# Row moments of a second normalisation, taken by ScalarE and GpSimd instead of VectorE, inside a top-k attention kernel

## What is computed

```python
x = x + attention(layernorm(x))      # 16 heads of 64, relative positions, top 32 scores of each row kept
x = x + ffn(layernorm(x))            # base product + low-rank experts gated by a softmax

def _layernorm(x, axis=-1, eps=1e-05):
    m = jnp.mean(x, axis=axis, keepdims=True)
    v = jnp.var(x, axis=axis, keepdims=True)
    return (x - m) / jnp.sqrt(v + eps)

# in attention, for each head:
top_vals = jax.lax.top_k(scores, TOPK)[0]          # TOPK = 32
threshold = top_vals[..., -1:]
scores = jnp.where(scores < threshold, -jnp.inf, scores)
attn = jax.nn.softmax(scores, axis=-1)             # then three powers of attn times v, weighted by alphas
```

## Time and profile before

| | us |
|---|---|
| median of 3 runs | 708.71 |
| lowest, highest | 706.1, 710.16 |
| the profiled execution, its own time | 707.67 |
| its span, first to last instruction | 705.7 |

### The profile page before, as it was taken

How to read it: one execution, slowest core, us unless ns; L and a number is a source line. 1 busy time by engine, 2 the same in 40 slices (tenths; PEclk the granted TensorE clock), 3 DMA queues, 4 the chain that set the end, 5 groups by cost and what they waited for, 6 DMA issues and landing times.

```text
span 705.7 us, 20962 instructions
## 1 busy us (share of the span) xinstructions
PE 655.9 (93%) x5780; PEld 510.2 (72%) x5780; DVE 676.5 (96%) x2813; ACT 619.9 (88%) x1774; POOL 552.6 (78%) x985
## 2 busy tenths in 40 slices
PE   4378999999999999999999999999999999999796
PEld 3256777777777777877777777777777777777664
DVE  6899999999999999999999999999999999999963
ACT  3678999989999899999999999998999999998753
POOL 1588898888878888888887888788887888888740
PEclk9779999999999999999999999999999999999999
DMA  6644444544554545454544544454545444545212
GB/s 202 189 117 145 143 142 147 149 123 144 165 156 140 149 135 154 135 154 137 152 137 139 151 144 146 132 157 134 155 126 163 135 139 145 151 136 154 69 47 59
DMA packets 148338, 98.72 MB, mean 140 GB/s; under 512 B 10624, under 2 KB 147968, under 8 KB 148096
## 3 DMA queue, kind: packets, MB, share of 16 engines
q1 hardware_dynamic: 147920, 97.32, 47.0%
q10 hardware_dynamic: 304, 0.08, 0.1%
HBM read 45.59 MB, written 51.77 MB: 138 GB/s over the span
## 4 chain that ended last, share of the span: by engine, by line
DVE 79%; issue 9%; PE 7%; POOL 2%; ACT 2%; DMA 1%; ACTq 0%; DVEq 0%; POOLq 0%; SPq 0%
DVE top L749 41%; DVE work L755 36%; PE ps_p L974 2%; DVE rinv L736 1%; POOL s_sb L331 1%; PE ps_y L994 1%; ACT a_sb L491 1%; DMA x_sb<-in_x 0%; DMA band_scratch<-band 0%; DVE stats L771 0%; PE ps_d L951 0%; PE ps_qk L896 0%; PE ps_p L920 0%; PE ps_d L942 0%; DMA skew<-band_scratch 0%
## 5 line engine op out<-in xcount | busy, mean ns | idle before, releaser
L749 DVE MAX8 top<-work 128x8 f32<-128x256 f32 x768 | 286.8, 418 | 0.0
L755 DVE MATCH_REPLACE8 work<-top,work 128x256 f32<-128x256 f32 x512 | 207.3, 416 | 0.0
L331 POOL TENSOR_TENSOR s_sb<-s_sb,pen 128x512 f32<-128x512 f32 x127 | 162.0, 1276 | 38.6 <-ACT pen L481 35.5
L336 POOL TENSOR_SCALAR a_sb<-a_sb,rinv 128x256 f32<-128x256 f32 x254 | 118.7, 478 | 53.0 <-DVE rinv L736 52.7
L491 ACT ACTIVATE a_sb<-s_sb,nmax 128x256 f32<-128x256 f32 x256 | 128.2, 502 | 27.9 <-POOL s_sb L331 19.2
L481 ACT ACTIVATE pen<-s_sb,limit 128x256 f32<-128x256 f32 x254 | 116.3, 511 | 19.7 <-POOL limit L318 19.6
L306 POOL TENSOR_TENSOR s_sb<-s_sb,skew 128x384 f32<-128x384 f32 x128 | 128.4, 1003 | 2.5 <-DMA skew<-band_scratch 2.5
L974 PE MATMUL ps_p<-aT,rows 128*64 128x256 f32 x1024 | 125.3, 386 | 0.4 <-ACT rows L555 0.2
L755 DVE MATCH_REPLACE8 work<-top,s_sb 128x256 f32<-128x256 f32 x256 | 103.6, 415 | 0.0
L749 DVE MAX8 top<-s_sb 128x8 f32<-128x256 f32 x256 | 95.1, 416 | 3.9 <-POOL s_sb L306 3.9
L882 PE MATMUL ps_a<-ident,a_sb 128*128 128x128 f32 x512 | 84.8, 289 | 13.1 <-POOL a_sb L336 12.9
(11 more groups left out here) (168 smaller groups left out, 1315.8 us busy)
## 6 DMA issues: line engine op xcount, KB each, us to landing
skew<-band_scratch SPq DMA_DIRECT2D x128, 192.0 KB, 2.7
diag_scratch<-a_sb SPq DMA_DIRECT2D x128, 192.0 KB, 2.3
band_scratch<-band SPq DMA_DIRECT2D x128, 191.0 KB, 3.3
diag<-diag_scratch SPq DMA_DIRECT2D x128, 128.0 KB, 2.2
wqkv<-in_wqkv SPq DMA_DIRECT2D x1, 1152.0 KB, 7.5
x_sb<-in_x SPq DMA_DIRECT2D x4, 256.0 KB, 4.7
wout<-in_wout SPq DMA_DIRECT2D x1, 512.0 KB, 5.5
out<-xn SPq DMA_DIRECT2D x1, 512.0 KB, 3.2
```

The source lines that it names most:

```text
L331: nc.gpsimd.tensor_tensor(s_sb[g % 4][:], s_sb[g % 4][:], pen[g % 2][:], ALU.subtract).then_inc(pen_added, 1)
L336: nc.gpsimd.tensor_scalar(a_sb[g % 3][:, t, :], a_sb[g % 3][:, t, :], rinv[g % 2][:, t:t + 1], 1.0, ALU.mult, ALU.mult).then_inc(normed, 1)
L749: nc.vector.max(m[:, t, 8 * n:8 * n + 8], src).then_inc(top_step, 1)
L755: nc.vector.match_replace(work[t][:, n % 2, :], m[:, t, 8 * n:8 * n + 8], src, LOW).then_inc(top_step, 1)
```

## The change

The moments of batches 0 to 6 leave VectorE. ScalarE now copies the projection one tile at a time with an accumulating output, which gives the row sums `ysum`. GpSimd scales them by -1/128 (`scale_sum`) and subtracts the mean of `x`, which the first normalisation left in `mv` (`second_mean`), so `shift` holds minus the mean of `y`. ScalarE then squares `y + shift` with an accumulating output (`squares`, one tile at the end of slot 5, one at the end of slot 6), which gives 128 times the variance in `ysq`. The steps after it keep their arithmetic. Because the squares are there only after slot 6, `second_variance` and `second_scale` move to slot 7 on GpSimd, and in GpSimd's list they stand ahead of `normalise(2q - 1)`. The second feed-forward product and its copy move from slot 3 to slot 4 on PE and ScalarE. Batch 7 is left as it was.

```diff
+            def scale_sum(b):
+                pool.wait_ge(yp_saved, T * (b + 1))
+                nc.gpsimd.tensor_scalar(ysum[:], ysum[:], -1.0 / DIM, 1.0, ALU.mult, ALU.mult).then_inc(ysum_scaled, 1)
+            def second_mean(b):
+                i = slice(T * b, T * (b + 1))
+                pool.wait_ge(ysum_scaled, b + 1)
+                nc.gpsimd.tensor_tensor(shift[:, i], ysum[:], mv[:, i, 0], ALU.subtract).then_inc(mean_done, 1)
             def second_variance(b):
                 i = slice(T * b, T * (b + 1))
-                pool.wait_ge(row_stats, 2 * TILES + 2 * T * (b + 1))
-                nc.gpsimd.tensor_scalar(rstd[:, i], mv[:, i, 1], EPS, 1.0, ALU.add, ALU.mult).then_inc(var2_done, 1)
-                nc.gpsimd.tensor_scalar(shift[:, i], mv[:, i, 0], -1.0, 1.0, ALU.mult, ALU.mult).then_inc(var2_done, 1)
+                pool.wait_ge(square_done, T * (b + 1))
+                nc.gpsimd.tensor_scalar(rstd[:, i], ysq[:, i], 1.0 / DIM, EPS, ALU.mult, ALU.add).then_inc(var2_done, 1)
...
             def second_steps(q):
                 b = q // NP - 1
+                if b >= 0 and q % NP == 4:
+                    add_projection(b)
                 if b >= 0 and q % NP == 5:
-                    second_variance(b)
-                if b >= 0 and q % NP == 6:
-                    second_scale(b)
+                    scale_sum(b)
+                    second_mean(b)
...
                 if on(q):
                     add_skew(2 * q + 1)
+                if q >= NP and q % NP == NP - 1:
+                    second_variance(q // NP - 1)
+                    second_scale(q // NP - 1)
                 if on(q - 1):
                     normalise(2 * q - 1)
...
             # ScalarE
-                if 0 <= b < INSIDE and q % NP in (2, 3):
-                    save_layer(b, q % NP - 2)
+                if 0 <= b < INSIDE and q % NP in (2, 4):
+                    save_layer(b, q % NP // 4)
             def save_projection(b):
                 act.wait_ge(proj_done, NP * (b + 1))
                 reach(act, y_done, b)
-                nc.scalar.copy(yp_sb[:].rearrange("p t d -> p (t d)"), ps_y[:, 0:T * DIM]).then_inc(yp_saved, 1)
+                reach(act, mean_done, b)
+                for t in range(T):
+                    nc.scalar.activation(yp_sb[:, t, :], ps_y[:, t * DIM:(t + 1) * DIM], ACT.Copy, scale=1.0,
+                                         accum_out=ysum[:, t:t + 1]).then_inc(yp_saved, 1)
+            def squares(b, t):
+                i = T * b + t
+                act.wait_ge(y_done, b + 1)
+                act.wait_ge(mean_done, b + 1)
+                nc.scalar.activation(yn[:, i, :], y_sb[:, i, :], ACT.Square, bias=shift[:, i:i + 1], scale=1.0,
+                                     accum_out=ysq[:, i:i + 1]).then_inc(square_done, 1)
+            def row_work(q):
+                b = q // NP - 1
+                if b >= 0 and q % NP == 3:
+                    save_projection(b)
+                if b >= 0 and q % NP in (5, 6):
+                    squares(b, q % NP - 5)
...
             # VectorE, in the loop over heads
-                q = g // 2
-                if g % 2 == 1 and q >= NP + 4 and q % NP == 4:
-                    row_moments(q // NP - 1)
...
             # PE
-                if 0 <= b < INSIDE and q % NP in (2, 3):
-                    layer(b, q % NP - 2)
+                if 0 <= b < INSIDE and q % NP in (2, 4):
+                    layer(b, q % NP // 4)
+                if 0 <= b < INSIDE and q % NP == 5:
+                    pe.wait_ge(layer_saved, T * (b + 1))
```

More of the change, by code:

```diff
@@ L116, in preln_attention_ffn @@
         halves = sb("halves", [P, T])
+        ysum = sb("ysum", [P, T])
+        ysq = sb("ysq", [P, TILES])
         eps = sb("eps", [P, 1])
@@ L161, in preln_attention_ffn @@
         proj_done, yp_saved, y_done, var2_done = sem("proj_done"), sem("yp_saved"), sem("y_done"), sem("var2_done")
+        ysum_scaled, mean_done, square_done = sem("ysum_scaled"), sem("mean_done"), sem("square_done")
         rstd2_done, shift_done, yn_done = sem("rstd2_done"), sem("shift_done"), sem("yn_done")
@@ L353, in scale_wout @@
                                             ALU.mult).then_inc(wk_done, 1)
+            def scale_sum(b):
[5 more added lines that the diff above has]
+                nc.gpsimd.tensor_tensor(shift[:, i], ysum[:], mv[:, i, 0], ALU.subtract).then_inc(mean_done, 1)
             def second_variance(b):
                 i = slice(T * b, T * (b + 1))
-                pool.wait_ge(row_stats, 2 * TILES + 2 * T * (b + 1))
-                nc.gpsimd.tensor_scalar(rstd[:, i], mv[:, i, 1], EPS, 1.0, ALU.add, ALU.mult).then_inc(var2_done, 1)
-                nc.gpsimd.tensor_scalar(shift[:, i], mv[:, i, 0], -1.0, 1.0, ALU.mult, ALU.mult).then_inc(var2_done, 1)
+                pool.wait_ge(square_done, T * (b + 1))
+                nc.gpsimd.tensor_scalar(rstd[:, i], ysq[:, i], 1.0 / DIM, EPS, ALU.mult, ALU.add).then_inc(var2_done, 1)
             def second_scale(b):
                 i = slice(T * b, T * (b + 1))
-                pool.wait_ge(var2_done, 2 * (b + 1))
+                pool.wait_ge(var2_done, b + 1)
                 nc.gpsimd.tensor_tensor(rstd[:, i], rstd[:, i], halves[:], ALU.pow).then_inc(rstd2_done, 1)
@@ L392, in add_projection @@
                 i = slice(T * b, T * (b + 1))
-                pool.wait_ge(yp_saved, b + 1)
+                pool.wait_ge(yp_saved, T * (b + 1))
                 nc.gpsimd.tensor_tensor(y_sb[:, i, :], y_sb[:, i, :], yp_sb[:], ALU.add).then_inc(y_done, 1)
@@ L415, in slot @@
                     scale_wout(q - 1, 0, 2)
-                if q >= NP + 4 and q % NP == 4:
-                    add_projection(q // NP - 1)
                 second_steps(q)
@@ L441, in _ @@
             add_skew(2 * q + 1)
+            second_variance(INSIDE)
+            second_scale(INSIDE)
             normalise(2 * q - 1)
@@ L619, in slot @@
                     save_rows(q)
-                if q >= NP + 3 and q % NP == 3:
-                    save_projection(q // NP - 1)
+                row_work(q)
             def gate_weights(i, a, e):
@@ L677, in _ @@
             save_third(q - 1)
-            act.wait_ge(row_stats, 4 * TILES)
+            act.wait_ge(row_stats, 2 * TILES + 2 * T)
             nc.scalar.activation(std[:, DONE:TILES], mv[:, DONE:TILES, 1], ACT.Sqrt, bias=eps[:, 0:1]).then_inc(last_root, 1)
@@ L767, in row_moments @@
             def row_moments(b):
-                n = 2 * TILES + 2 * T * b
+                n = 2 * TILES
                 dve.wait_ge(y_done, b + 1)
```

## The result

| | before | with the change |
|---|---|---|
| median, us | 708.58 (22 runs) | 712.08 (22 runs) |
| lowest to highest | 706.1 to 712.98 | 708.52 to 714.82 |
| ratio of times, 95% interval | | 1.0044 (1.0029 to 1.0059) |
| the profiled execution: own time, span | 707.67, 705.7 | 712.16, 710.3 |

The change costs 0.44%, which is 3.1 us; the two medians are 3.5 us apart. The forecast was +1.4 us (710.1): the sign and the range held, but more than twice that came.

What follows compares the result with a forecast made beforehand. VectorE was taken as the bound, the GpSimd and ScalarE round nearly as long. Per steady batch 0.90 us lost less 0.61 gained, +0.29; five batches +1.45, batch 0 nothing, batch 6 -0.1: 710.1 us, range 706.0 to 715.5.

Steps and rivals of the forecast that it cites:

- VectorE is the bound, and the round beside it all but as long: In the loop VectorE hardly waits; limit, ramp, penalty, exponential over GpSimd and ScalarE leave 0.04 to 0.21 us slack.
- Cushion: After VectorE's moments the other engines were 0.61 us ahead; that lead goes too, with no price given.
- Halves: ScalarE's projection copy as two accumulating halves: 0.54 us against 0.29, VectorE losing 0.21 in slot 4.
- Squares: ScalarE at the ends of slots 5 and 6: 0.39 us each; VectorE loses 0.07, next ramp 0.15 late in slot 7.
- Variance and power: GpSimd in slot 7 ahead of normalising: even ramp 0.51 us late; with the squares' 0.15, less 0.04 slack, VectorE loses 0.62.
- Scaled sum, mean, moved feed-forward product: GpSimd's small steps in slot 5 and the product moved to slot 4 are covered by waits and cost nothing.
- the rival by which the product delays PE: Moved product makes PE late for slot 4's rows: 0.2 to 0.4 us a batch, 712 us; chance 0.10.
- Batch 0 at nothing: VectorE's existing 0.45 us wait for an exponential absorbs gain and new delays alike: net 0 in batch 0.
- Batch 6: Squares cost nothing, variance and power about 0.3 us late: -0.61 + 0.21 + 0.3 = -0.1 us.
- Sum: Batches 1 to 5 +1.45 us, batch 0 nothing, batch 6 -0.1: about +1.4, median 710.1; own forecast's chance 0.60.
- Covered: Rival: ScalarE has more room and GpSimd's detour is absorbed, only the 4.3 us gain stays: 704.4; chance 0.08.
- Full lengths: Rival: ScalarE's accumulating passes don't overlap, halves cost 1.16 us, a square 0.58: 715.7; chance 0.22.

Runs made afterwards that it cites:

- e1: Kernel before, with the loop's moments of batches 0 to 6 left out on VectorE and nothing in their place: 705.07 us, ratio 0.9935.
- e3: Changed kernel with one plain 256-column projection copy instead of two accumulating halves, row sums taken as zero: 710.29 us, ratio 1.0018 to the kernel before.
- e4: Changed kernel without ScalarE's squares, the variance a constant: 710.28 us, ratio 1.0011 to the kernel before.
- e2: Changed kernel without GpSimd's variance and power in slot 7: 706.89 us, ratio 0.9978 to the kernel before.
- e7: Kernel before with only SP's list reordered, each fetch of diagonals one send later: 706.5 us, ratio 0.9988.
- e8: Changed kernel with SP's list reordered as in e7: 708.19 us, ratio 1.002 to the kernel before.
- e10: e1 with PE's transposes of the powers ahead of its projection in each slot: 708.48 us, ratio 0.9991 to the kernel before.
- e12: e10 with SP's list reordered as in e7: 702.61 us, ratio 0.9903 to the kernel before.

## Why the prediction came out as it did

- **VectorE is the bound, and the round beside it all but as long** held. The gain, 0.61 us a batch and 4.3 in all, is confirmed by e1: its period gives 7 x 0.47 = 3.3 us after 0.17 a batch has come back, and the runs give 3.8 (0.65%).
- **Cushion.** I wrote that the 0.61 us for which the others were ahead "goes too", and gave it no price. It has one: 0.17 us a batch at the rows in slot 4 (e1, e3). It is hidden in the changed kernel behind the halves' 0.21, so it did not move this result, but it caps what undoing a part brings.
- **Halves.** Pair 0.51 us measured against 0.54, slot 4's loss 0.21 against 0.21. The Trainium skill, page "ScalarE: Activation LUTs", section "What ACT_TABLE_LOAD costs", would by my estimate have made a half 0.20 us without the read. The rows show 0.17 (472.78 to 472.95) and 0.26 with the read.
- **Squares.** Price 0.39 us as predicted, 0.10 lost in slot 6 against 0.07. The term that failed is the carry into slot 7: 0.15 predicted, 0.03 measured (e4). Perhaps VectorE's own loss in slot 6 had made up for part of it; no run tells that apart.
- **Variance and power** is the mis-sized term: 0.51 - 0.04 = 0.47 us predicted, 0.73 measured without squares (e4), 0.69 by leaving them out (e2). The two instructions took what I said (0.90). I counted one hand-off of 0.11 and an overlap of 0.03, 0.98 in all; there are three gaps of 0.08 to 0.10 and no overlap, 1.17 in all. That is the 0.11 at the first one that I had kept for the upper bound, and some more. It is 0.19 of the 0.26 that were missing. The slot as a whole came nearer (0.62 against 0.76) only because the squares' carry was 0.12 too high: that was luck.
- **Scaled sum, mean, moved feed-forward product** cost nothing visible. ScalarE waits 0.38 for the rows in slot 4 of e3 and 0.42 in e1, which has no moved product, and 0.16 in the changed kernel: the rival by which the product delays PE falls. That its 712 is the time that was measured is chance.
- **Batch 0 at nothing** was wrong by 0.44 us. I had counted on its 0.45 wait absorbing everything, but that wait lay in one place: slot 7 loses 0.79 like the others, and 0.7 appear at divisions of slots 10, 11 and 13, where the steady batches lose nothing. In e7 and e8, without late sends, batch 0 costs 0.42 like any other. **Batch 6** came out at +0.1 against -0.1, because the last even division waits longer than the 0.3 I gave it. This is the timeline of VectorE in the last slot:

```profile
676.25 0.17 DVE L771 RECIPROCAL rinv<-rsum 128x2 f32<-128x2 f32 x1 [0.51 <-ACT a_sb L509]
```

- **Sum.** Steady 5 x 0.15 = 0.75 us, batch 0 0.44 and batch 6 0.2 are missing, 1.4 together; 1.4 + 1.4 = 2.8 against 3.1 by the ratio (3.5 by the medians; the interval of the ratio is 2.1 to 4.2). The profiled execution shows 4.6 because of the 1.7 us in heads 32 to 48, most likely of SP's round. I never read SP's list, and the prediction has no term for it: when it is late it shows up as a pause of PE.
- **The rivals.** Covered (704.4): out, slot 7 waits. Full lengths (715.7): out, start to start the halves take 0.51 and not 1.16.

What stays open: why SP's lag settles in some executions and not in others. That the 1.7 us of heads 32 to 48 are SP's rests on SP's timeline, on e8, where they are absent, and on the pair e10 and e12; no run produced them on purpose in the changed kernel, and late sends alone don't, as e3 shows. Of the 0.26 that variance and power cost beyond my sum, 0.07 is not in the three gaps; the trace of e4 shows 0.04 of it, the ramp following the normalising 1.15 us later and not 1.11.

## What to carry to other kernels

When an engine is the bound by some hundredths of a microsecond, a step moved off it pays only where the engine that takes it over already waits, and both ends of every new hand-off have to be moved together: the same instructions cost 1.07 us a batch at slot ends and 0.18 in the gaps, and 1.47 in one slot when only one end was moved. Here each small instruction put into GpSimd's list cost its length plus 0.1 us. Read slack at the consumer (how long its input has been ready when it starts), not busy shares. And read the queue that issues transfers as one more engine: when its round is as long as the bound's, its lag hardly drains.

## What was not expected of the hardware

**Executions differ by some us in their first slots.** The kernel before and e1 do the same up to head 16, and it starts at 103.0 us in one trace and at 105.2 in the other. So do e7 and e8, with 104.7 and 100.5. How much of the scatter of a kernel's runs (2 to 10 us) comes from there isn't shown: over the 12 runs of e8 the time falls as the mean granted clock rises (correlation -0.94), over the 35 of the kernel before beside e1 much less (-0.38). Windows of core 0 from 20 to 45 us (length, busy time and instructions of PE, weight load, VectorE, ScalarE and GpSimd, granted clock of PE, DMA share, GB/s), first of the kernel before:

```profile
20.00:45.00 25.00, 12.42 (x71) 9.12 (x68) 24.63 (x103) 15.47 (x44) 16.58 (x31) 0.66 0.56 153
```

then of e7, with the window behind it:

```profile
20.00:45.00 25.00, 11.76 (x64) 8.55 (x60) 24.81 (x103) 14.82 (x41) 16.36 (x31) 0.62 0.62 160
...
45.00:70.00 25.00, 20.51 (x160) 15.14 (x160) 23.20 (x97) 21.12 (x60) 21.02 (x41) 0.90 0.55 149
```

and of e8:

```profile
20.00:45.00 25.00, 13.06 (x90) 9.71 (x90) 24.96 (x106) 18.28 (x50) 17.68 (x33) 0.80 0.62 161
...
45.00:70.00 25.00, 21.13 (x192) 16.31 (x193) 25.00 (x106) 22.79 (x66) 22.71 (x43) 1.00 0.61 163
```

In each there is a stretch at the lower level, 1.2 GHz: about 27 to 44 us in most traces, 26.2 to 46.7 and 63.8 to 67.2 in e7, only 28.3 to 38.5 in e8. Where it is long, VectorE then waits at early divisions, 3.4 us in slots 1 to 5 of e7 (in the second window it is busy 23.20 of 25 us) and none in e8 (25.00 of 25). So single spans of kernels this close compare their starts as much as their loops; e7's span is 706.8 and e8's 704.9, while their medians stand the other way round. The period in full flow was the steadier measure.

**A transfer lands later right behind others.** Over all 14 traces the same 192 KB to `diag_scratch` land after a median of 2.3 us (2.0 to 4.9, nineteen in twenty under 4.0) when SP issued nothing in the 0.5 us before, and after 3.3 us (2.5 to 5.1) right behind two skews or bands.
